# Graph recommender on one core: the messages' destinations found during the sort instead of by look-ups in the first layer

## The reference

```python
for _ in range(3):
    x = segment_sum(vals[:, None] * x[cols], rows, num_segments=18750)
    acc = acc + x
light = acc / 4
```

## Time and profile before

| what | us |
|---|---|
| median of 3 runs | 5698.38 (5697.66 to 5706.33) |
| the profiled execution | 5699.68, span 5697.8 |
| DVE busy | 4895.9 (86%) |
| PE busy | 3586.0 (63%) |
| ACT busy | 2424.7 (43%) |
| POOL busy | 2322.5 (41%) |

### The profile page before, as it was taken

How to read it: one execution, slowest core, us unless ns; L and a number is a source line. 1 busy time by engine, 2 the same in 40 slices (tenths; PEclk the granted TensorE clock), 3 DMA queues, 4 the chain that set the end, 5 groups by cost and what they waited for, 6 DMA issues and landing times.

```text
span 5697.8 us, 200992 instructions
## 1 busy us (share of the span) xinstructions
PE 3586.0 (63%) x72493; PEld 3095.9 (54%) x72731; DVE 4895.9 (86%) x8588; ACT 2424.7 (43%) x3894; POOL 2322.5 (41%) x2074
## 2 busy tenths in 40 slices
PE   5500111111788888877768888777758888877767
PEld 4400111110777777766657777766657777766652
DVE  9999999999777777777789988877789889987778
ACT  0045556533444444430026656550026666650017
POOL 0044334410555555550017777770007777770000
PEclk9955555555787888879989999989989999989989
DMA  9940000000666666669977777769977777779999
GB/s 331 415 199 0 0 0 0 0 0 7 195 203 205 212 205 209 204 215 328 328 214 245 241 235 240 235 225 328 328 229 243 238 241 240 243 225 320 328 285 358
DMA packets 767571, 1210.54 MB, mean 212 GB/s; under 512 B 68253, under 2 KB 585278, under 8 KB 767120
## 3 DMA queue, kind: packets, MB, share of 16 engines
q1 hardware_dynamic: 646112, 835.98, 49.9%
q0 software_dynamic: 121088, 372.73, 16.9%
q10 hardware_dynamic: 304, 1.00, 0.1%
HBM read 658.19 MB, written 551.32 MB: 212 GB/s over the span
## 4 chain that ended last, share of the span: by engine, by line
DVE 33%; DMA 28%; issue 17%; PE 16%; POOL 3%; ACT 2%; DVEq 1%; SPq 0%; POOLq 0%; ACTq 0%
DMA ring<-posts 14%; DMA posts<-ring 12%; PE psum L1480 8%; DVE ring L1240 6%; DVE store L1020 6%; PE psum L1512 4%; DVE total L815 3%; POOL posts L729 3%; DVE store L998 3%; PE psum L1463 3%; DVE store L999 2%; DVE ring L1194 2%; DMA out<-new 2%; DVE ring L1282 1%; DVE new L1181 1%
## 5 line engine op out<-in xcount | busy, mean ns | idle before, releaser
L729 POOL DMA_INDIRECT posts<-ring x1884 | 1904.4, 1011 | 2015.6 <-DVE ring L1194 1454.0
L1480 PE MATMUL psum<-store,ring 128*128 x45216 | 2147.5, 205 | 497.1 <-DVE ring L1240 395.8
L1480 PEld LDWEIGHTS psum<-store,ring 128*128 128x128 bf16 x45216 | 1922.3, 105 | 719.5 <-issue 571.6
L655 ACT ACTIVATE ring<-new 128x512 bf16<-128x512 bf16 x942 | 594.4, 631 | 1289.4 <-DVE new L1181 1281.5
L657 ACT ACTIVATE new<-new 128x512 bf16<-128x512 uint8 x1884 | 1067.4, 613 | 0.0
L1240 DVE TENSOR_SCALAR ring<-ring,lane_f 128x1024 bf16<-128x1024 bf16 x1884 | 867.9, 502 | 10.2 <-DMA ring<-lanes_d 10.2
L1282 DVE TENSOR_TENSOR ring<-ring,wide_lane 128x1024 bf16<-128x1024 bf16 x948 | 613.3, 689 | 288.8 <-ACT ring L666 288.8
L1181 DVE TENSOR_TENSOR new<-psum,ring 128x512 f32<-128x512 f32 x942 | 645.9, 686 | 202.7 <-PE psum L1480 194.3
L711 POOL TENSOR_TENSOR ring<-store 128x1024 f32<-128x1024 f32 x157 | 370.2, 2358 | 798.7 <-DVE store L999 364.1
L1194 DVE TENSOR_TENSOR ring<-new 128x1024 bf16<-128x1024 bf16 x942 | 652.2, 692 | 36.0 <-ACT new L657 3.6
L1512 PE MATMUL psum<-ring 128*128 128x64 bf16 x11520 | 387.9, 194 | 169.9 <-DVE ring L1282 165.0
(11 more groups left out here) (225 smaller groups left out, 3156.1 us busy)
## 6 DMA issues: line engine op xcount, KB each, us to landing
ring<-lanes_d SPq DMA_DIRECT2D x471, 512.0 KB
ring<-posts SPq DMA_DIRECT2D x240, 772.0 KB, 6.7
store<-posts SPq DMA_DIRECT2D x234, 772.0 KB
posts<-store SPq DMA_DIRECT2D x2, 30880.0 KB, 166.4
posts<-store SPq DMA_DIRECT2D x2, 30108.0 KB, 128.2
out<-new SPq DMA_DIRECT2D x96, 500.0 KB, 8.4
posts<-ring POOLq DMA_INDIRECT x1884
new<-runs_d SPq DMA_DIRECT2D x78, 256.0 KB
```

The costliest lines, as they stand in the source:

```text
L655: nc.scalar.activation(msg_parts[:, 0, 4 * d:4 * d + 4, :], scaled_high[s], ACT.Copy).then_inc(s_high, 1)
L729: pool.indirect_dma_start(out=posts[:, :], out_offset=bass.IndirectOffsetOnAxis(ap=dring[:, h, c:c + 1], axis=0), in_=msg[:, n, :], in_off ...
L1480: last = pe.matmul(psum[:, d % 4, (n % 2 * BLOCK + b) * F:(n % 2 * BLOCK + b + 1) * F], of, xflat[:, bass.ds(at_d[c] * F + (k * XT + x * F ...
```

## The change

The destination of a block is its sorted position plus `delta` of its run, and `delta` is the same from one run's first block to the next run's. The new code writes `delta` (raised by 1 << 17, so that it is never zero) as a mark at each run's first block in a cleared array `places`, reads this back as 128 partitions by 628 blocks, and fills the zeros by scans that carry the last mark forward: first within each partition, then over the 128 partitions' last values in one row, and these back into the partitions. Empty runs have their marks sent to spare rows behind the array.

```diff
 # tables (DVE), in place of the split of delta into dparts and PE's two transposes of it
+            nc.vector.tensor_scalar(mark_at, start, 1.0 / BLOCK, float(OFFSET), ALU.mult, ALU.add)
+            ... 11 more on 74 partitions x 150 or less (spare rows, empty runs, values, casts)
+            nc.vector.tensor_copy(mark_at_i, mark_at).then_inc(s_tabled, 1)
 # SP: one write ahead of the clearing of posts; the rest behind the dummy keys (L489)
+            sp.dma_start(places[0:CHUNKS * P, :]..., blank[:, 0:CHUNKS]).then_inc(s_noplaces, 16)
+            sp.wait_ge(s_tabled, 1)
+            ... marks_at and marks_value out, 2 writes each; wait for all four (s_tabout, 64)
+            sp.dma_start(spot_i[:, :], marks_at...).then_inc(s_tabin, 16)
+            sp.dma_start(spot_v, marks_value...).then_inc(s_tabin, 16)
+            sp.wait_ge(s_placed, 16 * MARK_COLS)
+            sp.dma_start(marked, places...).then_inc(s_marked, 16)
+            ... filled's last column out, in as one row; row_out out, in as carry (128 numbers each)
+            sp.dma_start(dest_d.rearrange("o (p c) -> (o p) c", p=P), dest_i[:, :]).then_inc(s_destout, 16)
+            sp.wait_ge(s_destout, 16)
+            dest_v = dest_d.rearrange("o (c l) -> (o l) c", l=P)
+            for q in range(4):
+                c = slice(q * CHUNKS // 4, (q + 1) * CHUNKS // 4)
+                sp.dma_start(dest_m[:, c], dest_v[:, c], allow_slow_non_contiguous=True).then_inc(s_dest, 16)
 # POOL, in the loop over the sort's steps, behind greater_of(n)
+                if n == MARK_FIRST - 1:                       # MARK_FIRST = 10
+                    pool.iota(order_i, ...).then_inc(s_orders, 1)
+                    pool.wait_ge(s_noplaces, 16)
+                    pool.wait_ge(s_tabin, 32)
+                k = n - MARK_FIRST
+                if 0 <= k < MARK_COLS:                        # MARK_COLS = 87
+                    pool.indirect_dma_start(out=places[:, :], out_offset=...(ap=spot_i[:, k:k + 1], axis=0),
+                        in_=spot_v[:, k:k + 1], in_offset=None).then_inc(s_placed, 16)
 # DVE, ahead of steps 114, 119 and 124 of the sort
+            def fill_rows():          # waits for s_marked: is_equal and scan on 128x628
+            def fill_firsts():        # is_equal and scan on 1x129
+            def destinations():       # is_equal, multiply and add, add on 128x628
 # after the merge (DVE, SP)
-            link(nc.vector.tensor_scalar(bits_r, ..., 15, 255, ...))
-            nc.vector.tensor_copy(runs_b..., bits_r).then_inc(s_lanes, 1)
-            nc.vector.tensor_scalar(dest_m[:, :], order_i, lane_f[:, 0:1], None, ALU.add)
-            ... the four writes of runs_d
 # the first layer
-            run_hots, place, look_up, SP's reads of runs_r, and every wait on them
-            if layer == 0: for q in range(SPLITS): take(0, q)   # ahead of the loop
+            take(layer, d) within the first body, as in the other layers; s_dest awaited ahead of the layer
```

More of the change, by code:

```diff
@@ L181, in build @@
         start_i = table(640, W).bitcast(I32)
-        incl, blocks, delta = (table(800 + a * 160, RUNS) for a in range(3))
+        incl, blocks = (table(800 + a * 160, RUNS) for a in range(2))
+        delta = table(1120, W)
         each, run_f, key_f = (table(1300 + a * 960, PER_SUPER) for a in range(3))
@@ L496, in _ @@
                 sp.dma_start(by_row[P:ROWS_M, h * 1024:(h + 1) * 1024], lanes_b[h * HALF:(h + 1) * HALF, WIDE:MWIDE]).then_inc(s_lanesd, 16)
[L497 to L502, removed]
+            sp.wait_ge(s_lanesd, 64)
             sp.wait_ge(s_decoded, 1)
@@ L1039, in _ @@
                 k, j, way = STEPS[n]
+                if n == ROW_FIRST:
+                    fill_rows()
+                if n == ROW_NEXT:
+                    fill_firsts()
+                if n == DEST_AT:
+                    destinations()
                 if n in TURN:
@@ L1246, in send @@
                             n = min(8, 2 * pairs - 8 * h)
-                            if layer == 0:
-                                place(i, h, n)
                             refill(i, h, first, n)
-                        if layer and first and d < SPLITS:
+                        if first and d < SPLITS:
                             take(layer, d)
-                        if layer == 0 and j == 2:
-                            run_hots(i * 32 + 16 * (h + 2), i * 2 + (h + 1), REST if final and h == 1 else 8)
-                if layer == 0:
-                    for q in range(SPLITS):
-                        take(0, q)
-                    run_hots(16, None)
-                    send(0, True)
-                    with dve.Fori(1, BODIES - 1) as i:
-                        send(i, False)
-                    send(BODIES - 1, False, True)
-                    send(BODIES, False, pairs=REST // 2)
-                else:
-                    send(0, True)
-                    with dve.Fori(1, BODIES) as i:
-                        send(i, False)
-                    send(BODIES, False, pairs=REST // 2)
+                send(0, True)
+                with dve.Fori(1, BODIES) as i:
+                    send(i, False)
+                send(BODIES, False, pairs=REST // 2)
                 low_parts(BODIES, 7, -1)
@@ L1484, in sums @@
                             last.then_inc(s_sent, 1)
[L1485 to L1495 removed]
+                with pe.Fori(0, BODIES) as i:
+                    sums(i)
                 sums(BODIES, chunks=REST)
```

186 lines of the change are left out of this document (88 added, 98 removed).

## The result

The changed kernel takes **5491.4 us** in the median (5489.2 to 5493.7, 4 runs), beside 5698.0 of the kernel before (5696.5 to 5706.3, 4 runs): a ratio of 0.9634, 95% interval 0.9622 to 0.9645. Its profiled execution took 5490.8, with a span of 5488.9. The forecast was 5482, the range 5455 to 5555.

What follows compares the result with a forecast made beforehand. DVE bounds the sort; in the first message stage PE's look-ups stand in line with its gathers while DVE waits. Terms -242.5 - 1.7 + 0 + 13.5 + 8.7 + 5.0 + 0 = -217 gave 5482 us, range 5455 to 5555.

Steps and rivals of the forecast that it cites:

- The first message stage: First message stage without look-ups: runs at the later stages' price, 875 instead of 1117.5 us, 242.5 us gained (225 to 255).
- the 5 us for the copies: First message stage: seven `take`s are plain copies, each 0.7 us shorter than later layers' adds, 5 us in all.
- the second rival: First message stage: clock stays at 0.80 because of the sort, only DVE's 94 us go, total 5630; chance 0.06.
- The clock: First message stage: granted clock rises from 0.80 to over 0.9 once the look-up pauses are gone.
- POOL's wait: Sort, step 9: POOL waits for the marks' reads, step 10's subtraction starts at 380.2, 13.5 us lost (9 to 20).
- The scatters: Sort, steps 10 to 96: 87 scatters on POOL each hold DVE 0.1 us, 8.7 us lost (0 to 26).
- the first rival: Sort: scatters hold DVE for their whole length, 72 us instead of 8.7, total 5545; chance 0.09.
- The fills: Sort: DVE's operations that carry the marks forward all count, 5.0 us lost (4 to 7).
- The decoding: Decoding: three operations of 0.55 us go, 1.7 us gained.
- The tables: Tables: nine small DVE operations and a wait for PE transposes become twelve operations; 0, within 1 us.
- The load of* `dest_m`: Between sort and first layer: 80,384 separate 4-byte numbers load in 50 us, hidden, so 0.
- The third rival: Ahead of the first layer: `dest_m`'s load is late, 638 us at 127 ns a number, total 5646; chance 0.05.

Runs made afterwards that it cites:

- both_waits: Changed kernel with both engines' look-up parts and their mutual waits back in the first layer, without run-number reads and first add into `dest_m`: 5735.9 us, ratio 1.0019.
- mark16: Changed kernel with the marks' scatters starting at sort step 16 instead of 10: 5457.7 us, ratio 0.9590.
- dve_part: Changed kernel with only DVE's part of the look-ups back in the first layer, no waits between engines, copies ahead of the loop: 5502.3 us, ratio 0.9672.
- pe_spread_regs: pe_spread with matmul addresses worked out from each chunk's own, already loaded register instead of constants: 5517.9 us, ratio 0.9648.
- pe_regs: Changed kernel with only the register loads of PE's look-ups back in the first layer, no matmuls: 5522.6 us, ratio 0.9660.
- pe_mm: Changed kernel with only the 16 look-up matmuls per half body back, in one piece at constant addresses, no register loads: 5516.0 us, ratio 0.9643.
- pe_spread: pe_mm with its 16 constant-address matmuls placed two behind each chunk's gathers instead of in one piece: 5521.7 us, ratio 0.9660.
- pe_part: Changed kernel with only PE's look-ups back in the first layer, register loads and 16 matmuls per half body, result not awaited: 5650.9 us, ratio 0.9878.
- pe_one_address: pe_part with the two matmuls of a chunk sharing one address: 5566.2 us, ratio 0.9732.

## Why the prediction was right

*The first message stage.* Forecast -242.5 us (225 to 255), measured 1117.5 - 883.4 = -234.1. The step held: same code, same price, same clock. The size is 8.4 us too good. The three stages here differ by 4.5 us among themselves, and the 5 us for the copies did not show, though each `take` did become 0.7 us shorter, 0.85 instead of 1.55 us. In the four other runs whose message stages are the changed kernel's, the first stage was 0.1 to 5.1 us shorter than the mean of the later two, so a part of the 5 may be there. Where it saves nothing, the 71 us that DVE waits in this stage for scatters to land would explain it; that is not tested. That DVE is next, nine tenths busy, was half right: it is DVE together with the landing of POOL's scatters, as in the later stages.

*Why the look-ups cost so much.* The prediction took the whole size from the difference between stages, and said that PE's 166.5 us stand in line with the gathers while DVE waits. The experiments bear out the place and give the parts, which the prediction did not have: DVE's own work 27 us, PE's 126, 60 more only with both, and 25 (238 - 213) for what both_waits left out, the run numbers' reads and the add into `dest_m`. The 60 and the 25 are differences and no run takes them apart; the 25 also sets one chip's trace against another's. DVE's look-up work, which the second rival priced at 94 us, was worth 27.

*The clock.* Forecast over 0.9, measured 0.92. The stage has the same sort ahead of it, so the second rival (5630) is false. The prediction's sign of being right, a clock over 0.9 once the pauses are gone, came true; why the clock follows them is not shown.

*POOL's wait.* Forecast +13.5 us (9 to 20), measured 18.2 by the steps' starts, 17.8 by what mark16 gave back. The step came at 381.30 where 380.2 was forecast; the forecast's term counted only the late start and not the tail at step 12, where the minimum takes 4.10 us (388.97), another 3 us.

*The scatters.* Forecast +8.7 us (0 to 26), measured 0.35. The start was as forecast: POOL is let in at L1035's end, 1.78 us a scatter. The hold of 0.1 us on L1036 does not exist; its mean is 1239 ns, before 1238. So the first rival (5545) is false too (the prediction's paragraph on the skill calls it the second by mistake). The Trainium skill ("SBUF — State Buffer", section "Who interferes with whom") has a DVE instruction with two SBUF inputs and a GpSimd instruction that reads SBUF contend, and calls the ports that they share an exclusive lock; that whoever issues first has it for the whole instruction, it says of DVE's 2-port modes. The trace agrees on one side, where the scatter waits for L1035's end (1.78 us instead of 0.98) and L1035 for the subtraction's (4.10 us), and not on the other: L1036 runs beside a scatter that is under way (1.21 us at 673.75).

*The fills.* Forecast +5.0 us, measured 3.5. The operations were priced rightly, 4.8 us against 4.9 (the scan over 628 took 1.47 where 1.6 stood); that all of it counts was too strict, as DVE had idle time there. *The decoding*: forecast -1.7, measured about -2.1. *The tables*: 0, measured -0.1.

*The load of* `dest_m`. Forecast 50 us and hidden, measured 49.6 and hidden. The third rival is false. The Trainium skill ("VectorE: DVE Perf Modes", section "The three transpose paths") has a plain DMA that transposes by strides 19 times slower than the transposing one, for a large innermost stride at the destination; the estimate of 122 us that the prediction worked out from it is not borne out, as this load took less than half.

*The sum.* -234.1 + 18.2 + 0.4 + 3.5 - 2.1 - 0.1 = -214.2, and the other two message stages, 3.1 us longer together than before (883.3 + 878.9 against 885.1 + 874.0), make -211.1. The span fell by 208.9; the 2.2 between are spread over the rest. The forecast's -217 was 8 us too good. (5482.7 less the 1.3 gives 5481.4, so the forecast's 5482 stands 0.6 above its own sum.) Three terms were off by more than 3 us, the stage (8.4 too good), the wait (4.7 too good) and the scatters (8.4 too dear, which hid the first); the untouched stages' 3.1 came on top. That two errors of 8.4 us cancel is luck: with the scatters priced rightly the forecast would have been 17.7 us too good, and the result still inside the range.

## What to carry to other kernels

Work that one engine does in one piece ahead of its main work costs only what goes beyond its waits: sum those waits before pricing it. On PE, count the addresses worked out from registers, not only the matmuls: halving them brought back 73 of the 126 us that the piece cost. And where a wait stands in a queue that feeds the bound engine, put the first use a few steps later: six steps gave 18 us here for one constant.

## What the runs showed of the hardware

- Matmuls of 128x3 with an address worked out from a register each followed one another in 0.12 us (eight in 1.03 us, the last of which lasts 0.18); where two shared an address, eight took 0.55 us, and with constant addresses sixteen took 0.54 us. The register instruction ahead of each shows in the trace with 0.04 us.
- An indirect scatter of 128 numbers of 4 bytes, issued while DVE works with two SBUF inputs, waits for the end of that instruction (1.78 us instead of 0.98), but does not hold up the next such instruction (1239 ns in the mean, 1238 without the scatters), nor one that starts 0.4 us into a scatter (1.24 us at 663.25). POOL's own subtraction does hold it up: the minimum beside it took 2.20 and 4.10 us instead of 1.2.
- A load of 80,384 separate numbers of 4 bytes took 49.6 us from the first issue to the last landing, 9.9 ns per number and engine, with the DMA engines otherwise nearly idle.
- The granted clock, a mean over the levels of 1.2 and 2.4 GHz, was 0.92, 0.96 and 0.95 in first stages without the piece of look-ups (the changed kernel, dve_part, pe_spread_regs), 0.91 in those with the loads alone or the matmuls alone (pe_regs, pe_mm, pe_spread), and 0.82, 0.83 and 0.80 in those with the whole piece (pe_part, pe_one_address, both_waits), though PE was busy for 83 to 87% of these and 76 to 86% of the first three. The gathers' busy time was longer at the lower clock (729.5 us at 0.82, 698.6 at 0.91, in one run), so 29 of pe_part's 126 us lie there; how much of the rest is the piece and how much the clock is not settled.
